# Attention over experts: output projection and value projection each go one head later, directly in front of a block of value products

## The chip, the cores and the metric

One core of one Trainium2 chip runs the whole program. The metric is the device time of one execution in microseconds (us), the median of three runs. The profile is one further execution with the hardware profiler on. In it PE is TensorE (PEld its weight loads), DVE is VectorE, ACT is ScalarE, POOL is GpSimd and SP is SyncE, which issues the DMAs.

## What is computed

A network of four layers on 16 sequences of 256 tokens with 128 features; each layer is an attention and a feed-forward part, each behind a layer normalisation and added to `x`. Three of these parts are attentions with 16 heads of 8 features: that of layer 1, the feed-forward part of layer 2 (four expert attentions on the same tokens, each with its own weights, a mask of the tokens that chose it, and a gate), and the attention of layer 3 (with rotary tables). Cut to that, for one sequence and one set of weights:

```python
q, k, v = (x @ wq + bq), (x @ wk + bk), (x @ wv + bv)      # per head of 8 features
att = softmax(mask(einsum('bqhd,bkhd->bhqk', q, k) * scale))
y = einsum('bhqk,bkhd->bqhd', att, v).reshape(b, s, d)
out = out.at[...].add(gate * (y @ wo + bo))                # four experts: one such term each
```

## The kernel before

`attention8` carries out these three attentions: once for layer 1 (16 jobs, one for each sequence), and once for layers 2 and 3 together (64 jobs, sequence times expert, then 16 late jobs of layer 3). A job is one sequence under one set of weights. The five engines each run a list of steps; in step `at` an engine works on several jobs at different depths, and `s.has(off)` asks whether job `at + off` exists. A step goes over 16 heads, `u` = 0 to 15.

On PE, each head of a step gives one pair of matmuls of scores for job `at + 1` (`scores_part`, L596, into `psS`) and, beside them, one pair of transposed, shifted scores (`shifted_part`, L603, into `psT`), all on 49 or 51 rows of the array. DVE takes the row maxima of each `psS` bank (`maxima`, L831), ACT the exponentials of each `psT` bank (`exponential`, L754). `psS` and `psT` have three banks each (`SCORE_BANKS, SHIFTED_BANKS, MISC_BANKS = 3, 3, 1`), used in turn, so before a head's pair PE waits until the maxima and the exponentials of the head three before it are done (`max_done`, `exp_done`, L616 and L622).

Between the heads stand larger blocks of PE, at places written out by hand in `step` (L692 on): the projections to q and k after head 0 (L582, L583), the turning of the output after head 3 (L664), four blocks of value products `prob_values(s, 0..3)` after heads 3, 6, 10 and 14 (L645, 16 matmuls each that write 32-column strips of the array), the turning of the maxima after head 4 (L671) and of y after head 6 (L679), the output projection `project_out` after head 9 (L686 for the bias, L689), and the value projection `project_v` after head 13 (L589). When late jobs are underway, a second projection follows head 3 and one more transpose ends the step.

All the blocks except the value products write one shared PSUM bank in a fixed order: q and k, o, m, y, out, v. Each of them waits until the previous one was taken out (`misc_taken`, in `fill`, L571). `add_output` on DVE (behind the maxima of head 10) takes the output projection: two instructions at L855 for the expert jobs, one at L859 for the others. `write_values` on ACT (behind the exponential of head 13) takes the value projection; a POOL copy of tokens (`tokens`, L953) waits for that, and the q projection of the next step waits for the copy. SP's queue and POOL's other steps wait for none of the two projections.

PE takes its matmuls in the order of its list, and so do DVE, ACT and POOL with theirs: an instruction that waits holds up all behind it.

Of the kernel before, what the change touches and what calls it, by code (L numbers as in the profile page):

```python
# [414 lines left out]
def attention8(nc, m, name, w, weights=1, masked=False, then=None):  # L415
# [12 lines left out]
    with ExitStack() as ctx:  # L428
# [45 lines left out]
        def of(s, off):  # L474

            return then if s.late(off) else w
# [89 lines left out]
        def _(pe):  # L566
# [7 lines left out]
            def project_qk(s, kind, wq, wk):  # L574
                if s.late(3) and then:
                    wait_taken(pe, s, "n", 3)
                    xc = m.xT16[:, s.batch(3), :]
                else:
                    pe.wait_ge(tokens_ready, s.n(3, 1, 1))
                    xc = xcur[:, s.quarter(3), :]  # L580
                ps, full = fill(s, kind, 3)
                pe.matmul(ps[:, 0:SEQ], wq[:, s.expert(3), :], xc, start=True, stop=True)  # L582
                pe.matmul(ps[:, SEQ:2 * SEQ], wk[:, s.expert(3), :], xc, start=True, stop=True).then_inc(full, 1)  # L583
# [22 lines left out]
            def score_pair(s, u):  # L606

                off, h = shifted_head(u)
                if s.has(1):
                    if u == 0:  # L610
                        if s.at == -1:
                            norm.wait(pe, GROUPS - 1)
                        pe.wait_ge(stack_ready, s.n(1, stack_inc, stack_inc))
                    back = score_bank(s, u)[1]
                    if s.known(1, 1) or u >= back:
                        pe.wait_ge(max_done, s.n(1, HEADS, u + 1 - back))  # L616
                if s.has(off):
                    if h == 0:
                        pe.wait_ge(maxrow_ready, s.n(0, 32, 32))
                    back = shifted_bank(s, u)[1]  # L620
                    if s.known(off, 1) or h >= back:
                        pe.wait_ge(exp_done, s.n(off, HEADS, h + 1 - back))  # L622
                for t in range(2):
                    if s.has(1):
                        a = scores_part(s, u, t)
                        if t == 1:
                            a.then_inc(scores_ready, 1)
                    if s.has(off):
                        b = shifted_part(s, u, t)
                        if t == 1:  # L630
                            b.then_inc(shifted_ready, 1)
# [26 lines left out]
            def turn_output(s):  # L658
                pe.wait_ge(oT_ready, s.n(-2, 2, 2))
                ps, full = fill(s, "o", -2)  # L660
                for t in range(2):
                    for half in range(2):
                        c = (2 * t + half) * P
                        mm = pe.transpose(ps[:, c:c + P], oT[:, half, t * P:(t + 1) * P], m.identity[:, :])  # L664
                mm.then_inc(full, 1)

            def turn_max(s):
                pe.wait_ge(negmax_ready, s.n(0, 1, 1))
                ps, full = fill(s, "m", 0)
                for t in range(2):  # L670
                    mm = pe.transpose(ps[0:2 * HEADS, 0:P].bitcast(BF16)[:, t * P:(t + 1) * P],  # L671
                                      negmax[:, t, :, :, :].rearrange("p g a h -> p (g a h)"), m.identity_bf[:, :])
                mm.then_inc(full, 1)

            def turn_y(s):
                wait_taken(pe, s, "o", -2)
                ps, full = fill(s, "y", -2)
                for t in range(2):
                    mm = pe.transpose(ps[:, t * P:(t + 1) * P], y[:, t, :], m.identity[:, :])  # L679
                mm.then_inc(full, 1)  # L680
# [11 lines left out]
            def step(s):  # L692
                for u in range(HEADS):
                    score_pair(s, u)
                    if u == 0 and s.has(3):
                        project_qk(s, "qk", of(s, 3).wq, of(s, 3).wk)
                    if u == 3 and s.has(3) and then and s.late(3):
                        project_qk(s, "qk2", then.wq2, then.wk2)
                    if u == 3 and s.has(-2):
                        turn_output(s)  # L700
                    if u == 3 and s.has(-1):
                        prob_values(s, 0)
                    if u == 4 and s.has(0):
                        turn_max(s)
                    if u == 6 and s.has(-1):
                        prob_values(s, 1)
                    if u == 6 and s.has(-2):
                        turn_y(s)
                    if u == 9 and s.has(-2):
                        project_out(s)  # L710
                    if u == 10 and s.has(-1):
                        prob_values(s, 2)
                    if u == 13 and s.has(0):
                        project_v(s)
                    if u == 14 and s.has(-1):
                        prob_values(s, 3)

                if then and s.has(5) and s.late(5):
                    turn_late(s)
                for g in groups_at.get(s.at, ()):  # L720
                    norm.turn(pe, g)
                if masked and s.at == -3:
                    route.project(pe)
                if masked and s.at == -2:
                    route.count(pe)
# [5 lines left out]
        def _(act):  # L731
# [48 lines left out]
            def copy_yT(s):  # L780
                ps, taken = wait_full(act, s, "y", -2)
                if s.known(-2, 1):
                    wait_taken(act, s, "out", -3)
                act.activation(yT[:, :], ps[:, 0:SEQ], ACT.Copy).then_inc(taken, 1)

            def step(s):
                for u in range(HEADS):
                    if u == 1 and s.has(-2):
                        copy_oT(s, -2, 1)
                    if u == 1 and s.has(3):  # L790
                        copy_qk(s, "qk", 0)
                    if u == 4 and s.has(3) and then and s.late(3):
                        copy_qk(s, "qk2", 1)
                    if u == 6 and s.has(0):
                        copy_max(s)
                    if u == 7 and s.has(-1):
                        copy_oT(s, -1, 0)
                    if u == 7 and s.has(-2):
                        copy_yT(s)
                    exponential(s, u)  # L800
                    if u == 7 and then and s.at in STATS_AT:
                        late_roots(STATS_AT.index(s.at))
                    if u == 13 and s.has(0):
                        write_values(s)

                if s.at == -4:
                    norm.root(act)
                if then and s.has(5) and s.late(5):
                    ps, taken = wait_full(act, s, "n", 5)
                    act.activation(m.xT16[:, s.batch(5), :], ps[:, 0:SEQ], ACT.Copy).then_inc(taken, 1)  # L810
                for g in groups_at.get(s.at, ()):
                    norm.keep(act, g)
                if masked and s.at == -3:
                    route.keep_logits(act)
                if masked and s.at == -2:
                    route.keep_mask(act)
# [5 lines left out]
        def _(dve):  # L822
# [95 lines left out]
            def step(s):  # L918
                for u in range(HEADS):
                    if s.has(1):  # L920
                        maxima(s, u)
                    if then and s.at in STATS_AT:
                        late_statistics(STATS_AT.index(s.at), u)
                    if u == 12 and then and s.has(5) and s.late(5):
                        late_normalise(s)
                    if u == 2 and s.has(-2):
                        normalise(s)
                    if u == 10 and s.has(-2):
                        add_output(s)
                    if u == 15 and s.has(-2) and (s.late(-2) or s.expert(-2) == weights - 1):  # L930
                        output_stats(s)

                if s.at == -4:
                    norm.statistics(dve)
                if masked and s.at == -4:
                    for g in range(GROUPS):
                        norm.normalise(dve, g)
                    route.choose(dve)
                elif not masked:
                    for g in groups_at.get(s.at, ()):  # L940
                        norm.normalise(dve, g)
# [1171 lines left out]
```

## Time and profile before

| | us |
|---|---|
| median of three runs | 2327.8 |
| the three runs | 2325.37 to 2330.94 |
| profiled execution, its own time | 2331.32 |
| its span, first to last instruction | 2329.6 |
| PE busy | 2085.3 (90%) |
| DVE busy | 1814.9 (78%) |
| ACT busy | 1460.6 (63%) |
| POOL busy | 695.9 (30%) |
| mean granted clock of TensorE | 0.954 |

The profiled execution took 3.5 us more than the median, and 1.7 us of it lie around the span. The layer-1 attention runs from about 590 to 812 us of the span, that of layers 2 and 3 from about 1079 to 2160 us. A busy PE in this profile is not PE at its peak, since the ends of matmuls are modelled; their starts are what to read.

### The profile page before, as it was taken

To read this page: it belongs to the slowest core of one execution; us is meant where nothing else is said; L and a number is where in the kernel's file an instruction comes from. 1 tells how busy PE (TensorE), PEld (TensorE's weight loads), DVE (VectorE), ACT (ScalarE), POOL (GpSimd) and SP (SyncE) were. 2 spreads that over 40 slices of the span, in tenths; PEclk is the share of its full clock that TensorE was granted. 3 is DMA by queue.
4 is the path that set the end of the run, shared out by engine and by line. 5 is a ranking of instruction groups with operands and counts; after the bars stand their busy time and mean duration, and the time that the engine had idled before them with its cause. 6 is when DMAs were issued, how large, how long until landed. Compare 5 with 4: busy or idle time off the path is not lost. (4 is left out here: it accounts for less than half of the span.)

```text
span 2329.6 us, 66565 instructions
## 1 busy us (share of the span) xinstructions
PE 2085.3 (90%) x21573; PEld 1237.6 (53%) x21573; DVE 1814.9 (78%) x4556; ACT 1460.6 (63%) x3730; POOL 695.9 (30%) x1221
## 2 busy tenths in 40 slices
PE   5999999987899887756999999999999888888798
PEld 4777777755355454542545555555555444444355
DVE  7878877755689647986889998899999877776564
ACT  3565555632488723322878888888888777777331
POOL 2111111100343101322434434434433355552110
PEclk9999999998799988776999999999999999999899
DMA  5000000000434100003343443444344333331000
GB/s 164 2 2 2 2 2 2 2 1 15 137 124 128 40 1 1 1 0 97 121 129 124 129 131 124 128 132 131 128 129 132 113 98 111 98 102 53 1 19 19
DMA packets 198398, 167.48 MB, mean 72 GB/s; under 512 B 15445, under 2 KB 178198, under 8 KB 198198
## 3 DMA queue, kind: packets, MB, share of 16 engines
q1 hardware_dynamic: 198198, 164.90, 22.4%
q8 instruction: 114, 1.87, 0.3%
q14 instruction: 86, 0.70, 0.1%
HBM read 85.42 MB, written 77.63 MB: 70 GB/s over the span
## 5 line engine op out<-in xcount | busy, mean ns | idle before, releaser
L831 DVE TENSOR_REDUCE a_rowmax<-a_psS 128x2 f32<-128x512 f32 x1536 | 964.1, 681 | 141.4 <-PE a_psS L596 137.0
L754 ACT ACTIVATE a_probs<-a_psT 128x512 f32<-128x512 f32 x1536 | 830.5, 601 | 228.9 <-PE a_psT L603 228.8
L596 PE MATMUL a_psS<-stackk,stackq 49*128 49x256 bf16 x3072 | 498.2, 278 | 46.6 <-DMA stackq<-a_negmaxT 14.2
L603 PE MATMUL a_psT<-stackq,stackk 51*128 51x256 bf16 x3072 | 481.9, 273 | 2.1 <-ACT a_probs L754 1.9
L645 PE MATMUL a_psO<-a_probs,values 128*32 128x256 f32 x6144 | 412.8, 386 | 1.4 <-ACT a_probs L754 1.4
L596 PEld LDWEIGHTS a_psS<-stackk,stackq 49*128 49x128 bf16 x3072 | 220.1, 95 | 296.8 <-DVE a_rowmax L831 116.5
L645 PEld LDWEIGHTS a_psO<-a_probs,values 128*32 128x32 f32 x6144 | 160.8, 109 | 144.8 <-issue 51.2
L1175 ACT ACTIVATE a_probs<-a_psS,a_negmax 128x256 f32<-128x256 f32 x256 | 121.1, 473 | 182.8 <-DVE a_negmax L1199 182.8
L603 PEld LDWEIGHTS a_psT<-stackq,stackk 51*128 51x128 bf16 x3072 | 216.9, 94 | 19.3 <-ACT a_probs L754 8.1
L1059 POOL TENSOR_TENSOR a_vr<-a_v,a_rsum 128x256 f32<-128x256 f32 x128 | 79.8, 623 | 392.3 <-DVE a_rsum L1260 371.9
L953 POOL COPY a_xcur<-xT 128x256 f32 (+1 forms) x80 | 31.7, 396 | 467.8 <-ACT values L778 371.7
L1197 DVE CUSTOM_DVE_ANT_0 a_psS<-a_psS,causal 128x256 f32<-128x256 f32 x256 | 114.4, 447 | 72.3 <-PE a_psS L1081 60.3
L982 POOL TENSOR_TENSOR a_parts<-a_rest,a_parts 128x512 bf16<-128x512 f32 x96 | 111.1, 1158 | 17.3 <-POOL a_parts L980 17.3
L992 POOL TENSOR_SCALAR a_negmax<-a_rowmax 128x16 bf16<-128x16 f32 x192 | 45.0, 252 | 232.2 <-DVE a_rowmax L831 180.4
L978 POOL TENSOR_TENSOR a_rest<-a_raw,a_parts 128x512 f32<-128x512 f32 x80 | 92.6, 1157 | 14.8 <-POOL a_parts L976 14.8
L1077 PE MATMUL a_psS<-a_qT,a_kT 64*128 64x256 f32 x512 | 90.5, 429 | 5.3 <-DVE a_qT L1208 2.9
L1177 ACT ACTIVATE a_probs<-a_psS,a_negmax 128x128 f32<-128x128 f32 x256 | 93.4, 365 | 0.0
L664 PE MATMUL a_shared<-identity,a_oT 128*128 128x128 f32 x384 | 62.2, 285 | 32.9 <-ACT a_raw L744 29.3
L1412 DVE TENSOR_TENSOR f_hidden<-f_silu,f_up 128x512 f32<-128x512 f32 x48 | 32.9, 685 | 73.5 <-ACT f_silu L1393 73.5
L1393 ACT ACTIVATE f_silu<-f_gate 128x512 f32<-128x512 f32 x48 | 28.7, 597 | 94.5 <-PE f_up L1365 94.5
L1091 PE MATMUL a_psQ<-xT,l_wq 128*64 128x256 f32 x512 | 84.0, 406 | 1.0 <-PEq L154 1.0
L1199 DVE CUSTOM_DVE_ANT_0 a_psS<-a_psS,causal 128x128 f32<-128x128 f32 x256 | 84.4, 330 | 0.0
(305 smaller groups left out, 3892.6 us busy)
## 6 DMA issues: line engine op xcount, KB each, us to landing
a_scratch<-a_parts SPq DMA_DIRECT2D x192, 192.0 KB, 2.4
stackq<-a_scratch SPq DMA_DIRECT2D x192, 192.0 KB
stackk<-a_scratch SPq DMA_DIRECT2D x192, 192.0 KB
a_scratch<-a_parts SPq DMA_DIRECT2D x192, 128.0 KB, 2.3
a_scratch<-a_parts SPq DMA_DIRECT2D x192, 64.0 KB, 1.9
stackq<-a_negmaxT SPq DMA_DIRECT2D x192, 8.0 KB
x<-in_x SPq DMA_DIRECT2D x4, 512.0 KB, 6.4
out<-x SPq DMA_DIRECT2D x8, 256.0 KB, 2.3
```

The lines of the kernel that those rows point to most:

```text
L596: return pe.matmul(psS[score_bank(s, u)[0]][:, t * SEQ:(t + 1) * SEQ], stackq[r:r + MAX_ROW, b, pr, t * P:(t + 1) * P], stackk[r:r + MAX_R ...
L603: return pe.matmul(psT[shifted_bank(s, u)[0]][:, t * SEQ:(t + 1) * SEQ], stackk[r:r + ZERO_ROW, b, pr, t * P:(t + 1) * P], stackq[r:r + ZE ...
L645: mm = pe.matmul(psO[SLOT * j:SLOT * (j + 1), half, :], values[:, s.parity(-1), t, VALUE_AT + SLOT * (8 * i + 4 * half + j) - 9 * i:VALUE_ ...
L754: act.activation(probs[:, h, :], psT[shifted_bank(s, u)[0]][:, :], ACT.Exp, scale=of(s, off).exp_scale).then_inc(exp_done, 1)
L831: dve.tensor_reduce(rowmax[:, s.parity(1), u, :], psS[score_bank(s, u)[0]][:, :].rearrange("p (t k) -> p t k", t=2), AX_X, ALU.max).then_i ...
L978: pool.tensor_tensor(rest[:, :, :], whole, parts[:, :, 0, :], ALU.subtract).then_inc(rest_ready, 1)
L982: pool.tensor_tensor(parts[:, :, 2, :], rest[:, :, :], parts[:, :, 1, :], ALU.subtract).then_inc(parts_ready, 1)
L1077: pe.matmul(psS[a][h][:, 0:SEQ], kT[r, a, 0:P], qT[r, a, :], start=True, stop=True, tile_position=(64 * h, 0), skip_group_check=True)
L1175: act.activation(probs[:, a, h, 0:SEQ], psS[a][h][:, 0:SEQ], ACT.Exp, scale=-1.0, bias=negmax[:, a, 2 * h:2 * h + 1], accum_out=sums[:, a, ...
L1177: act.activation(probs[:, a, h, SEQ:384], psS[a][h][:, SEQ:384], ACT.Exp, scale=-1.0, bias=negmax[:, a, 2 * h + 1:2 * h + 2], accum_out=su ...
L1197: dve.tensor_tensor_reduce(out=psS[a][h][:, 0:SEQ], in0=psS[a][h][:, 0:SEQ], in1=m.causal[:, :], scale=-1.0, scalar=-NEG, op0=ALU.add, op1 ...
L1199: dve.tensor_tensor_reduce(out=psS[a][h][:, SEQ:384], in0=psS[a][h][:, SEQ:384], in1=m.causal[:, 0:P], scale=-1.0, scalar=-NEG, op0=ALU.ad ...
```

## The change

Three calls on PE, ACT and DVE move one head later. `project_out` moves from behind head 9 to behind head 10, where `prob_values(s, 2)` follows it in the same turn of the loop. `project_v` moves from behind head 13 to behind head 14, where `prob_values(s, 3)` follows it. The two readers move with them: `write_values` behind the exponential of head 14, `add_output` behind the maxima of head 11. No instruction is added or removed, and the shared bank's order stays.

```diff
@@ -706,11 +706,11 @@
                         prob_values(s, 1)
                     if u == 6 and s.has(-2):
                         turn_y(s)
-                    if u == 9 and s.has(-2):
+                    if u == 10 and s.has(-2):
                         project_out(s)
                     if u == 10 and s.has(-1):
                         prob_values(s, 2)
-                    if u == 13 and s.has(0):
+                    if u == 14 and s.has(0):
                         project_v(s)
                     if u == 14 and s.has(-1):
                         prob_values(s, 3)
@@ -800,7 +800,7 @@
                     exponential(s, u)
                     if u == 7 and then and s.at in STATS_AT:
                         late_roots(STATS_AT.index(s.at))
-                    if u == 13 and s.has(0):
+                    if u == 14 and s.has(0):
                         write_values(s)
 
                 if s.at == -4:
@@ -925,7 +925,7 @@
                         late_normalise(s)
                     if u == 2 and s.has(-2):
                         normalise(s)
-                    if u == 10 and s.has(-2):
+                    if u == 11 and s.has(-2):
                         add_output(s)
                     if u == 15 and s.has(-2) and (s.late(-2) or s.expert(-2) == weights - 1):
                         output_stats(s)
```

## Rows read from the trace of the kernel before

**Rows 1.** Busy time by stretch (two answers): stretch, its length, each engine's busy us, PEclk, DMA.

```profile
core 0: us, PE busy (x) PEld busy (x) DVE busy (x) ACT busy (x) POOL busy (x), PEclk, DMA share, GB/s
1500.00:1512.20 12.20, 11.98 (x149) 6.40 (x149) 11.09 (x22) 10.38 (x24) 4.86 (x10) 1.00 0.42 130
...
1840.00:2090.00 250.00, 219.23 (x2510) 118.37 (x2506) 193.83 (x381) 188.32 (x421) 131.75 (x190) 1.00 0.33 104
```

**Rows 2.** Timeline of PE, heads 7 to 15: start, length, operation, count.

```profile
1504.03 0.28 PE L596 MATMUL a_psS<-stackk,stackq 49*128 49x256 bf16 x1
1504.14 0.27 PE L596 MATMUL a_psS<-stackk,stackq 49*128 49x256 bf16 x1
...
1504.59 0.27 PE L596 MATMUL a_psS<-stackk,stackq 49*128 49x256 bf16 x1
1504.79 0.28 PE L686 MATMUL a_shared<-l_bo_parts,ones_bf 128*128 128x256 bf16 x1
1504.91 0.61 PE L689 MATMUL a_shared<-l_wo,a_yT 128*128 128x128 f32 x4
1505.45 0.28 PE L596 MATMUL a_psS<-stackk,stackq 49*128 49x256 bf16 x1
...
1505.57 0.27 PE L596 MATMUL a_psS<-stackk,stackq 49*128 49x256 bf16 x1
...
1505.77 1.07 PE L645 MATMUL a_psO<-a_probs,values 128*32 128x256 f32 x16
1506.78 0.28 PE L596 MATMUL a_psS<-stackk,stackq 49*128 49x256 bf16 x1
...
1507.37 0.27 PE L596 MATMUL a_psS<-stackk,stackq 49*128 49x256 bf16 x1
...
1507.57 0.71 PE L589 MATMUL a_shared<-l_wv,a_xcur 128*128 128x128 f32 x4
1508.22 0.28 PE L596 MATMUL a_psS<-stackk,stackq 49*128 49x256 bf16 x1
...
1508.54 1.07 PE L645 MATMUL a_psO<-a_probs,values 128*32 128x256 f32 x16
1509.54 0.28 PE L596 MATMUL a_psS<-stackk,stackq 49*128 49x256 bf16 x1
```

**Rows 3.** Timeline of DVE in the same stretch.

```profile
1504.45 0.69 DVE L831 TENSOR_REDUCE a_rowmax<-a_psS 128x2 f32<-128x512 f32 x1 [0.48 <-PE a_psS L596]
...
1506.85 0.60 DVE L855 SCALAR_TENSOR_TENSOR x<-a_shared,gate,x 128x128 f32 x2
1507.37 0.68 DVE L831 TENSOR_REDUCE a_rowmax<-a_psS 128x2 f32<-128x512 f32 x1
```

**Rows 4.** Timeline of PE in narrow looks: last output matmul, last transpose, value products.

```profile
1505.24 0.28 PE L689 MATMUL a_shared<-l_wo,a_yT 128*128 128x128 f32 x1
...
1500.37 0.27 PE L664 MATMUL a_shared<-identity,a_oT 128*128 128x128 f32 x1
...
1500.57 0.42 PE L645 MATMUL a_psO<-a_probs,values 128*32 128x256 f32 x4
```

**Rows 5.** Timelines of PE and DVE, step 1 of layers 2 and 3 (no output yet).

```profile
1112.72 0.28 PE L596 MATMUL a_psS<-stackk,stackq 49*128 49x256 bf16 x1
...
1113.28 0.27 PE L596 MATMUL a_psS<-stackk,stackq 49*128 49x256 bf16 x1
1113.92 0.27 PE L596 MATMUL a_psS<-stackk,stackq 49*128 49x256 bf16 x1 [0.37 <-DVE a_rowmax L831]
...
1113.15 0.69 DVE L831 TENSOR_REDUCE a_rowmax<-a_psS 128x2 f32<-128x512 f32 x1 [0.17 <-PE a_psS L596]
```

**Rows 6.** One line's instructions, all 32 of them: min/median/max ns, first and last start.

```profile
L859 DVE TENSOR_TENSOR x<-a_shared,x x32: 384/412/425, 636.2 to 2162.3; 128x256 f32<-128x256 f32 x24, 128x256 f32 x8
```

**Rows 7.** Timelines of ACT, POOL and PE, same step: value projection's way on.

```profile
1504.49 2.06 ACT L754 ACTIVATE a_probs<-a_psT 128x512 f32<-128x512 f32 x4
...
1508.68 0.42 ACT L778 ACTIVATE values<-a_shared 128x256 f32<-128x256 f32 x1
...
1509.44 0.40 POOL L953 COPY a_xcur<-xT 128x256 f32 x1 [5.11 <-ACT values L778]
...
1510.09 0.70 PE L582 MATMUL a_shared<-a_xcur,l_wq 128*128 128x256 f32 x2
```

**Rows 8.** Who waited for whom, whole run: us in total, times, longest.

```profile
PE a_psS L596 <- DMA stackq<-a_negmaxT: 14.2, 12, 3.1
```

**Rows 9.** Timeline of PE: waits for the shared bank, in two late steps in sequence.

```profile
1929.97 0.63 PE L664 MATMUL a_shared<-identity,a_oT 128*128 128x128 f32 x4 [1.09 <-ACT a_raw L744]
...
1945.26 0.63 PE L664 MATMUL a_shared<-identity,a_oT 128*128 128x128 f32 x4 [1.09 <-ACT a_raw L744]
```

## The prediction

> **What bounds the kernel now.** I read the stretches first, then the timeline of PE in one step of the layer-2 loop, then DVE and ACT in the same 12 us, and last the waits of the whole run. The stretches show a step of 12.20 us in which PE is busy for 11.98 us, DVE for 11.09 and ACT for 10.38 [rows 1]. So PE sets the pace, but DVE is only 0.9 us behind it and any time in which DVE starves is near to being on the path. PE runs at the full 2.4 GHz (granted 1.00), and still does in the late steps, where it is busy for 219 of 250 us [rows 1] with waits as long as 1.09 us in them [rows 9]; so short waits of PE, such as I expect below, don't bring the clock down.
>
> The timeline of PE [rows 2] is to be read by starts. I count from the first score matmul of head 7 (1504.03) and call the heads H7, H8 and so on. Three heads (H7, H8, H9) stand together; the last matmul of H9 starts at 0.56. Then the bias of the output projection at 0.76, the projection itself at 0.88, H10 at 1.42, value products at 1.74, H11 at 2.75. Again three heads stand together (H11, H12, H13, the last at 3.34), then the value projection at 3.54, H14 at 4.19, value products at 4.51, and H15 at 5.51. Nothing in it is a wait for a bank. Note the group size: three heads, and there are three banks.
>
> DVE [rows 3] starts the maxima of H7 at 0.42, after 0.48 us of waiting for PE: it has nothing left to do when H7 arrives. That instruction ends at 1.11 (0.42 + 0.69). The maxima of H8, H9, H10 follow without a gap; then the two L855 instructions fill 2.82 to 3.42, and the maxima of H11 start at 3.34.
>
> **The change part by part.**
>
> *What it removes: one change of tile shape for each move.* Between two score matmuls of a group lie 0.11 us from start to start (1504.03 to 1504.14 [rows 2]). Where the kind of matmul changes, it is about 0.20: H9's last to the bias 0.20, H10's last to the value products 0.20 [rows 2], the last output matmul (1505.24) to H10 0.21 [rows 2, 4]. The order "projection, then value products" has a row too, in the block after head 3: the last transpose on the full array starts at 1500.37 and the value products at 1500.57, again 0.20 [rows 4]. So before: 0.20 (H9 to projection) + 0.21 (projection to H10) + 0.20 (H10 to products) = 0.61. After: 0.11 (H9 to H10) + 0.20 (H10 to projection) + 0.20 (projection to products) = 0.51. Each move gives back 0.10 us of PE, two of them 0.20 us in a step.
>
> The Trainium skill says the same of this place: TensorEngine Tiling (Array Packing), section Key Properties, has "Changing tiling mode (not just tile) drains the TensorE". The trace agrees with about 0.1 us for a change. By that rule alone the kernel would get faster; this is my first rival.
>
> *What it adds: a fourth head in a group of three banks.* After the change H10 comes directly behind H9. PE could issue it at 0.67 (0.56 + 0.11), but its bank is that of H7, and the maxima of H7 end only at 1.11. DVE can't have them earlier, since it starts them as soon as H7 is there. The trace before has this very order in step 1, where no output exists yet and heads 7 to 10 stand together [rows 5]: H7 starts at 1112.72, H9's last at 1113.28, DVE starts at 1113.15 and ends at 1113.84, and H10 starts at 1113.92, 1.20 after H7 and 0.08 after the end of its maxima, with the wait put down to DVE. I take 1.20. The exponentials free the other bank no later (ACT starts four of them at 0.46, about 0.6 each [rows 7], so the first ends near 1.06). What waits behind H10 on PE is everything: projection, products, H11.
>
> *The new timetable, first half.* H10 at 1.20, its second matmul at 1.31; bias at 1.51 (+0.20); projection at 1.63 (+0.12), its last matmul at 1.96 (+0.33, from 1504.91 to 1505.24); products at 2.16 (+0.20); H11 at 3.17 (+1.01, as 1505.77 to 1506.78). Before, H11 came at 2.75: **+0.42**. The 0.66 us of projection used to cover the wait for H7's maxima; now nothing does.
>
> *Second half.* DVE has finished H10's maxima by about 2.9 (0.42 + 4 x 0.6) and starves until H11 is there. The output's reader, which used to fill that hole, now stands behind H11's maxima. These start at 3.59 (3.17 + 0.42) and end at 4.28. H14 needs that bank: 4.36 (+0.08), while PE was ready for it near 3.87. Its second matmul is at 4.48 (+0.12), and the value projection could start at 4.68 (+0.20). But it writes the shared bank, which is free only when DVE's reader is through: L855 starts at 4.19 (3.59 + 0.60, the pace of the maxima), takes 0.60 for the two [rows 3], ends at 4.79, and lets the value projection go at 4.87 (+0.08). Value products 0.65 later (as v to H14 now, 1507.57 to 1508.22) at 5.52, H15 1.00 later at 6.52. Before it was 5.51: **+1.01 us a step**. Where the reader is the single L859, 0.41 us [rows 6], it ends at 4.60, the value projection goes at 4.68, just as PE is ready, and H15 comes at 6.33: **+0.82 us a step**.
>
> *From H15 on* the order is the old one, all of it shifted. Two things could be late next. The q projection waits for the token copy on POOL, which waits for ACT to take v. Now: v at 1507.57 (last matmul near 1508.0), ACT takes it at 1508.68, behind other exponentials, for 0.42; POOL copies at 1509.44 for 0.40; q starts at 1510.09, 0.25 after the copy's end [rows 2, 7]. After: v at 4.87 is complete about 0.7 later; ACT, whose exponential of H14 starts at about 5.1 and runs for 0.6, takes it at about 5.65, to 6.07; POOL (+0.34) copies from 6.41 to 6.81; PE is ready for q at 7.07 (6.52 + 0.55, as 1509.54 to 1510.09). So it is hidden with some 0.2 us to spare; uncovered it costs what it overruns, to be bounded by one more exponential ahead of it, 0.5 us minus those 0.2, in each step. On ACT only the exponential of H15 stands behind the moved reader, and it waits for H15 anyway. On DVE the maxima of H12 to H14 stand behind L855; H15 needs H12's maxima, which end near 5.5, in time. No DMA is issued by what moves; SP and the other steps of POOL only follow the shift.
>
> *What it gives back.* Head 12 now and then waits for the DMA that brings the maxima, 12 times in the run, 14.2 us together [rows 8]. Heads 12 come 0.42 later, so up to 12 x 0.42 = 5 us of these vanish (bounds 0 and 14.2; I take 5).
>
> *The sum.* Steps with both moves and scores: 13 for layer 1 (steps 2 to 14, L859), 64 with an expert's output (steps 2 to 65, L855), 13 late ones (66 to 78, L859). 64 x 1.01 + 26 x 0.82 = 86 us, less 5: **+81 us**. The profiled execution would go from 2331.3 to 2412; it was 3.5 us above the median, so the median goes from 2327.8 to **2409 us**.
>
> The Trainium skill points this way also: Perfetto Trace Analysis, section Optimization Strategy, reads the same gap repeating on the engine that should be saturated as a sign of too little PSUM for the next tile. The trace before shows that gap only in a step such as that of rows 5.
>
> **The rivals.**
>
> *Faster by the saved tile changes alone.* If H7's maxima were done when PE reaches H10, 90 steps x 0.20 = 18 us would be gained: 2310 us. For it: the 0.20 rows. Against it: DVE would have to end 0.5 us sooner than it does, and it starts when H7 arrives. It decides from the point where the wait for a bank is under 0.10 us at each place.
>
> *Only the first wait counts.* If the later start of H11 gives DVE time to be ahead at H14 and the output is read in time, a step loses 0.42 - 0.10 = 0.32: 29 us, less 5: 2352. Against it: DVE starves before H11, so H11's maxima can't be early.
>
> *No change.* The waits would have to go where PE waits anyhow. In the loop that is 0.22 us of 12.20 [rows 1]; the late steps have more, but in front of H4, ahead of the moves. Against it is all of the timetable.
>
> *More than forecast.* The way v, values, tokens, q overruns by 0.3 us a step: 90 x 0.3 = 27 more, 2436.
>
> **How the numbers follow.** Forecast (both waits, 2378 to 2430) 0.80; first wait alone 0.06; overrun 0.05; faster 0.05; no change 0.04. The range: without the wait for L855 all steps would cost 0.82, 90 x 0.82 - 5 = 69, 2397; with all 14.2 us of the DMA waits gone too, 60, 2388; I go 10 further down for waits that overlap in part. Upward, with no DMA wait saved 2414, and 0.18 us a step for half of the overrun, 16, gives 2430. So 2378 to 2430. Faster by over 0.2% (about what a measurement can tell, 4.7 us) 0.05, within it 0.04, slower 0.91.
>
> **What would show it.** Right: on PE a wait of about 0.5 us in front of H10's and H14's scores, put down to the maxima of H7 and H11; DVE idle for about 0.6 us in front of H11's maxima; projections that start 0.20 after a score and products 0.20 after a projection; the value projection waiting for L855; steps of about 13.2 us in the loop and about 16.1 in late steps (15.29 now, 1929.97 to 1945.26 [rows 9]). Wrong: H10 less than 1 us after H7, or H15 less than 6 us after H7. If the bank waits are there but the step isn't longer, the timetable missed a slack; if steps are above 13.4, look at the token copy.

## The result, and the profile after

The changed kernel takes 2397.67 us (median of 4 runs, 2395.80 to 2399.49), the kernel before 2328.23 us beside it (median of 4 runs, 2325.37 to 2330.94): 1.0306 times as long, 95% interval 1.0291 to 1.0320. That is 69.4 us slower; the forecast was 2409 us, 81 us slower, in a range of 2378 to 2430. The profiled execution took 2397.04 us with a span of 2395.3, so it went up by 65.7 us against the profiled execution of before. Its mean clock is the same (0.955 after, 0.954 before).

The first look is at one step of the layer-2 loop in the stretches view of the changed kernel (length, then busy us of PE, PE's weight load, DVE, ACT and POOL, then the granted clock, the DMA share and GB/s). It answers to [rows 1]:

```profile
core 0: us, PE busy (x) PEld busy (x) DVE busy (x) ACT busy (x) POOL busy (x), PEclk, DMA share, GB/s
1502.00:1515.25 13.25, 12.16 (x150) 6.67 (x150) 11.24 (x22) 10.46 (x24) 5.10 (x10) 1.00 0.38 121
```

The step has become 1.05 us longer, and PE, DVE and ACT are busy in it for nearly what they were. PE's idle time rose from 0.22 to 1.09 us. So nothing got dearer: PE waits, at full clock.

Where it waits stands in the timeline of PE in that step (start, length, operation, and in brackets the idle time before it and who ended it). It answers to [rows 2], from the first score matmul of H7 at 1506.04 on:

```profile
1506.04 0.28 PE L596 MATMUL a_psS<-stackk,stackq 49*128 49x256 bf16 x1
...
1506.60 0.27 PE L596 MATMUL a_psS<-stackk,stackq 49*128 49x256 bf16 x1
...
1507.24 0.27 PE L596 MATMUL a_psS<-stackk,stackq 49*128 49x256 bf16 x1 [0.37 <-DVE a_rowmax L831]
...
1507.35 0.27 PE L596 MATMUL a_psS<-stackk,stackq 49*128 49x256 bf16 x1
...
1507.57 0.28 PE L686 MATMUL a_shared<-l_bo_parts,ones_bf 128*128 128x256 bf16 x1
1507.69 0.61 PE L689 MATMUL a_shared<-l_wo,a_yT 128*128 128x128 f32 x4
1508.23 1.07 PE L645 MATMUL a_psO<-a_probs,values 128*32 128x256 f32 x16
1509.23 0.28 PE L596 MATMUL a_psS<-stackk,stackq 49*128 49x256 bf16 x1
...
1510.43 0.27 PE L596 MATMUL a_psS<-stackk,stackq 49*128 49x256 bf16 x1 [0.37 <-DVE a_rowmax L831]
...
1510.92 0.71 PE L589 MATMUL a_shared<-l_wv,a_xcur 128*128 128x128 f32 x4
1511.56 1.07 PE L645 MATMUL a_psO<-a_probs,values 128*32 128x256 f32 x16
1512.57 0.28 PE L596 MATMUL a_psS<-stackk,stackq 49*128 49x256 bf16 x1
...
1513.11 0.70 PE L582 MATMUL a_shared<-a_xcur,l_wq 128*128 128x256 f32 x2
```

Read it by starts. H9's last score matmul stands at 0.56 after H7's first, H10 at 1.20: a gap of 0.64 us where 0.11 would do, so 0.53 us lost (the bracket says 0.37, since it counts from the modelled end of the matmul before). H14 has the same gap (from 1509.80, left out above, to 1510.43). Both waits are put down to the maxima. The value projection begins 0.38 after H14's last matmul (1510.54, left out above) instead of 0.20: that is the wait for DVE's reader of the output.

The same step on DVE, as [rows 3]:

```profile
1506.47 2.48 DVE L831 TENSOR_REDUCE a_rowmax<-a_psS 128x2 f32<-128x512 f32 x4 [0.48 <-PE a_psS L596]
1509.66 0.69 DVE L831 TENSOR_REDUCE a_rowmax<-a_psS 128x2 f32<-128x512 f32 x1 [0.71 <-PE a_psS L596]
1510.27 0.60 DVE L855 SCALAR_TENSOR_TENSOR x<-a_shared,gate,x 128x128 f32 x2
1510.78 1.88 DVE L831 TENSOR_REDUCE a_rowmax<-a_psS 128x2 f32<-128x512 f32 x3
```

DVE does four maxima and then sits idle for 0.71 us before H11's, where the two L855 instructions used to stand; they now come behind H11's maxima, and the value projection waits for them.

Over the whole run the waits have changed so (engine and line that waited, who ended it: us in total, times, longest). First the kernel before, then the changed one:

```profile
PE a_psS L596 <- DVE a_rowmax L831: 11.4, 19, 1.3
PEld a_shared L589 <- DVE x L855: 9.9, 47, 0.2
PE a_psS L596 <- issue: 4.7, 6, 1.9
```

```profile
PE a_psS L596 <- DVE a_rowmax L831: 74.5, 190, 0.9
PEld a_shared L589 <- DVE x L855: 23.2, 64, 0.4
PE a_psS L596 <- DMA stackq<-a_negmaxT: 4.5, 2, 2.5
PE a_psS L596 <- issue: 0.5, 2, 0.4
```

Two waits a step in some 90 steps make most of the 190; 19 were there before. The third line after answers to [rows 8]: 14.2 us of waits for the DMA became 4.5.

### The profile page after: what moved, and what is told of

It is laid out like the page before. It is cut to its first block and busy times, and to the rows that moved or that the text cites. A ratio compares the mean times of both kernels' runs of the same rounds, so it can differ in the third digit from the quotient of the medians.

```text
span 2395.3 us, 66551 instructions
## 1 busy us (share of the span) xinstructions
PE 2096.1 (88%) x21559; PEld 1244.0 (52%) x21573; DVE 1822.0 (76%) x4556; ACT 1460.9 (61%) x3730; POOL 698.3 (29%) x1221
## 5 line engine op out<-in xcount | busy, mean ns | idle before, releaser
L754 ACT ACTIVATE a_probs<-a_psT 128x512 f32<-128x512 f32 x1536 | 815.4, 600 | 298.6 <-PE a_psT L603 298.6
L596 PE MATMUL a_psS<-stackk,stackq 49*128 49x256 bf16 x3072 | 491.8, 277 | 94.1 <-DVE a_rowmax L831 74.5
L603 PE MATMUL a_psT<-stackq,stackk 51*128 51x256 bf16 x3072 | 477.0, 273 | 4.9 <-ACT a_probs L754 4.7
L596 PEld LDWEIGHTS a_psS<-stackk,stackq 49*128 49x128 bf16 x3072 | 225.7, 95 | 359.6 <-DVE a_rowmax L831 172.2
L664 PE MATMUL a_shared<-identity,a_oT 128*128 128x128 f32 x384 | 62.2, 285 | 32.9 <-ACT a_raw L744 28.9
```

The source lines that it names most:

```text
L596: return pe.matmul(psS[score_bank(s, u)[0]][:, t * SEQ:(t + 1) * SEQ], stackq[r:r + MAX_ROW, b, pr, t * P:(t + 1) * P], stackk[r:r + MAX_R ...
L603: return pe.matmul(psT[shifted_bank(s, u)[0]][:, t * SEQ:(t + 1) * SEQ], stackk[r:r + ZERO_ROW, b, pr, t * P:(t + 1) * P], stackq[r:r + ZE ...
L754: act.activation(probs[:, h, :], psT[shifted_bank(s, u)[0]][:, :], ACT.Exp, scale=of(s, off).exp_scale).then_inc(exp_done, 1)
```

## The experiments

The theory: each move puts four heads in front of three banks, so PE waits for the maxima (twice a step), and the late reader of the output adds a third wait. Every kernel was timed together with the kernel before, which stood at 2328.1 to 2328.4 us.

**One part at a time.** The first takes the changed kernel and gives DVE's reader its old place:

```
-                    if u == 11 and s.has(-2):
+                    if u == 10 and s.has(-2):
                         add_output(s)
```

> The changed kernel with add_output put back behind the maxima of head 10, so that the output's reader on DVE runs in the hole in front of head 11's maxima. My theory (the value projection waits for L855 through the shared bank): its start comes 0.18 us earlier in each of 64 steps, 0.20 behind head 14's last score instead of 0.36; 64 x 0.18 = 12 us less than the changed kernel's 2397.7, so 2386. The two bank waits in front of heads 10 and 14 stay. Rival (the value projection is held by something else): no difference, 2398.

It took 2387.04 us (1.0251, 1.0224 to 1.0279), about 11 us less than the changed kernel. On DVE the L855 pair fills the hole again, in front of the maxima of H11 (timeline of DVE):

```profile
1506.39 0.60 DVE L855 SCALAR_TENSOR_TENSOR x<-a_shared,gate,x 128x128 f32 x2
1507.18 2.48 DVE L831 TENSOR_REDUCE a_rowmax<-a_psS 128x2 f32<-128x512 f32 x4 [0.19 <-PE a_psS L596]
```

No wait of the value projection for L855 is left, and the waits for the banks are untouched (74.7 us, 190 times). So the late reader costs about 11 us, and the rest is the banks.

The second moves only the output projection, from the kernel before:

```
-                    if u == 9 and s.has(-2):
+                    if u == 10 and s.has(-2):
                         project_out(s)
```

> The kernel before with the output projection alone moved behind head 10; add_output stays behind the maxima of head 10, the value projection stays behind head 13. My theory (head 10 waits for head 7's bank): head 11 comes 0.44 us later and nothing else waits, so H15 is 0.44 later than before in 90 steps, 40 us, less some 16 us of DMA waits in front of head 12 that vanish: 2352. Rival (the saved tile change decides, the bank wait is hidden): 90 x 0.10 less, 2319.

2350.72 us (1.0095, 1.0066 to 1.0124), so +22.6, as the theory has it. One wait a step appears, in front of H10 (timeline of PE, then the waits of the whole run):

```profile
1510.94 0.28 PE L596 MATMUL a_psS<-stackk,stackq 49*128 49x256 bf16 x1 [0.42 <-DVE a_rowmax L831]
```

```profile
PE a_psS L596 <- DVE a_rowmax L831: 43.0, 105, 1.3
```

The third moves only the value projection:

```
-                    if u == 13 and s.has(0):
+                    if u == 14 and s.has(0):
                         project_v(s)
...
-                    if u == 13 and s.has(0):
+                    if u == 14 and s.has(0):
                         write_values(s)
```

> The kernel before with the value projection and write_values alone moved behind head 14. My theory (head 14 waits for head 11's bank by itself): DVE has the maxima of head 11 done at 4.02 us after head 7, head 14 goes at 4.10 instead of 3.45, head 15 at 6.07 instead of 5.51: 0.56 us a step, 50 us in 90 steps, and head 12 comes no later within its step, so few DMA waits vanish: 2370 to 2378. Rival (head 14's wait arises only because head 11 is late in the changed kernel): 90 x 0.10 less, 2319.

2358.53 us (1.0132, 1.0106 to 1.0157), so +30.4: the mechanism was right, the size was not. The wait stands in front of H14 (again the timeline of PE and the waits of the whole run):

```profile
1508.18 0.28 PE L596 MATMUL a_psS<-stackk,stackq 49*128 49x256 bf16 x1 [0.50 <-DVE a_rowmax L831]
```

```profile
PE a_psS L596 <- DVE a_rowmax L831: 46.8, 97, 1.1
PE a_psS L596 <- DMA stackq<-a_negmaxT: 8.5, 6, 3.6
```

Most steps of the loop grew by 0.57 us, as the expectation worked out (0.56). But the 26 steps with L859 grew by 0.45 only. In every fourth step of the loop a wait of 0.28 us in front of H0 went away, which comes from the turn of the loop ("The steps", below). And H12 was held up by 9.8 us in all by starts, where before it was 24.7 ("The give-back", below). Adding up: 22.6 + 30.4 + the 11 of the reader = 64 of the 69.4 us.

**The readers' time.** If the wait is for the maxima, shorter maxima must make it shorter. Two kernels, one from each side, let DVE and ACT read half of each bank (the expectation says what is left out):

```
-   act.activation(probs[:, h, :], psT[...][:, :], ...)
+   act.activation(probs[:, h, 0:SEQ], psT[...][:, 0:SEQ], ...)
...
-   dve.tensor_reduce(rowmax[...], psS[...][:, :].rearrange("p (t k) -> p t k", t=2), ...)
+   dve.tensor_reduce(rowmax[...], psS[...][:, :].rearrange("p (t k) -> p t k", t=2)[:, :, 0:P], ...)
```

> The kernel before with half of the work per score bank on its two readers: the maxima are taken over half of the keys, and the exponential is taken for half of the columns (the value products read that half twice). PE's work and every wait stay. Every theory: the step is paced by PE, so 2315 to 2330.

> The changed kernel with the same halved maxima and exponentials. My theory (head 10 and head 14 wait until the readers have left the bank): the maxima take about 0.41 us, the exponential about 0.39; head 10 goes at about 0.97 after head 7 instead of 1.20, head 15 at about 6.02 instead of 6.53, so a step costs 0.51 more than before instead of 1.01 (0.38 instead of 0.82 where L859 reads): 64 x 0.51 + 26 x 0.38 = 42 us over half_before, less up to 10 us of DMA waits: 32 to 42 over it. Rival (the new neighbourhood on PE costs the time, not the readers): as between the whole kernels, 69 us over half_before.

They took 2307.23 us (0.9921, 0.9898 to 0.9944) and 2348.67 us (1.0094, 1.0073 to 1.0115). The first came out lower than the 2315 to 2330 expected: most steps of its loop take 12.21 us as before, but the wait in every fourth step is gone, late steps take 15.07 instead of 15.28, and H12 is late by 17 us in all instead of 24.7. The difference, 41.4 us, is in the range of the theory (32 to 42) and far from the 69 that the change would have cost if the readers' time didn't matter. The second of them in the timelines of PE and of DVE (H7 at 1502.26):

```profile
1503.25 0.27 PE L596 MATMUL a_psS<-stackk,stackq 49*128 49x256 bf16 x1 [0.16 <-DVE a_rowmax L831]
```

```profile
1502.69 1.42 DVE L831 TENSOR_REDUCE a_rowmax<-a_psS 128x2 f32<-128x256 f32 x4 [1.16 <-PE a_psS L596]
```

H10 comes 0.99 after H7 instead of 1.20, and the wait is 0.16 instead of 0.37. DVE waits for 1.16 us before these maxima, so it is far from busy, and PE waits for it all the same. What counts is the time from a head's scores to the end of its maxima, not DVE's load. In the changed kernel that is 0.43 us until the maxima start and 0.69 for them, and H10 follows 0.08 later. These two runs don't tell the two readers apart, since both were halved. The traces do in part: the exponential that frees the other bank ends 0.06 us before the maxima, so by these rows shorter maxima alone could gain no more than that at each wait, an estimate that no run tests.

**The DMA's share.** H12 needs the maxima that a DMA brings. ACT copies them out at head 6; at head 5 the DMA starts earlier. From the kernel before, and from the changed one:

```
-                    if u == 6 and s.has(0):
+                    if u == 5 and s.has(0):
                         copy_max(s)
```

> The kernel before with one change of another kind: ACT copies the maxima (copy_max) in front of the exponential of head 5 instead of head 6, so that SP sends them some 0.45 us earlier. My theory (in the kernel before, head 12 often waits for that DMA, and the changed kernel lost less than I had summed because its head 12 comes later): these waits vanish here too, 14 to 18 us less than before, 2312. Rival (the waits are of the DMA's load and not of its start, or other steps take them over): 2328.

> The changed kernel with copy_max in front of the exponential of head 5, as in max_copy_early. My theory (the changed kernel has almost no waits left for the DMA in front of head 12, which is why it lost 69 us and not 81): nothing to gain, 2397, and it stands 79 us over max_copy_early, which is the price of the bank waits without that give-back. Rival (the copy helps wherever it is): 10 us less than the changed kernel, 2388.

From the kernel before it gives 2318.09 us (0.9958, 0.9943 to 0.9973): about 10 us faster than before, and the fastest kernel of this study that does all the work. The waits of this kernel:

```profile
PE a_psS L596 <- DVE a_rowmax L831: 9.3, 18, 1.0
PE a_psS L596 <- DMA stackq<-a_negmaxT: 8.8, 7, 2.8
PE a_psS L596 <- issue: 1.8, 4, 0.8
```

These three lines fell by 2.1, 5.4 and 2.9 us, 10.4 together. The direction was right, the size (2312 expected) too large, since 7 of the 12 DMA waits stayed. From the changed kernel the same edit gives 2395.58 us (1.0301, 1.0278 to 1.0324), nothing beyond the measurement: there the later H12 has already taken the gain. Against the better kernel the change therefore costs 77.5 us.

**Is the saved change of tile shape to be had at all?** The same neighbourhood (projection directly in front of products) can be made the other way, by taking the products one head earlier, so that the groups stay at three heads:

```
-                    if u == 10 and s.has(-1):
+                    if u == 9 and s.has(-1):
                         prob_values(s, -1, 2)
-                    if u == 13 and s.has(0):
+                    if u == 12 and s.has(0):
                         project_v(s)
-                    if u == 14 and s.has(-1):
+                    if u == 13 and s.has(-1):
                         prob_values(s, -1, 3)
...
-                    if u == 13 and s.has(0):
+                    if u == 12 and s.has(0):
                         write_values(s)
...
-                    if u == 10 and s.has(-2):
+                    if u == 9 and s.has(-2):
                         add_output(s)
```

> The kernel before with the value products moved to the output projection instead of the other way round: prob_values(2) directly behind project_out after head 9, project_v after head 12, prob_values(3) after head 13, add_output and write_values behind the maxima of head 9 and the exponential of head 12. The same change of tile is saved (one in a step: score, projection, products, score), but the groups of scores stay 3, 3, 1, 3 and no head waits for a bank. My theory (the bank, not the neighbourhood, costs the time): 90 x 0.10 = 9 us less than before, 2319, if the DMA of the maxima is in time; but head 12 comes about 0.15 us earlier in its step, so more waits for that DMA eat some of it: 2319 to 2330, with no step above 12.5 but for those waits. Rival (projections next to value products cost time in themselves, or the four turns about them disturb DVE): slower than before by half of the change, 2360.

> The same move of the value products, together with copy_max in front of head 5's exponential, so that the DMA in front of head 12 starts 0.45 us earlier. My theory: the saved tile change shows in full, 90 x 0.10 = 9 us less than copy_max alone (2318), so 2309, and faster than the kernel before by 0.8%. Rival (the step is bound by DVE or by the exchange through the shared bank as soon as PE gets shorter): no less than copy_max alone, 2318.

Alone it took 2338.69 us (1.0042, 1.0023 to 1.0061), with the earlier copy of the maxima 2328.70 us (1.0008, 0.9993 to 1.0022). Both miss: 10 us slower than without the move, where a gain was expected. The timeline of PE in the second says where the gain goes (its last line is of the kernel before, for the same place):

```profile
1502.70 0.28 PE L596 MATMUL a_psS<-stackk,stackq 49*128 49x256 bf16 x1
...
1508.62 0.70 PE L582 MATMUL a_shared<-a_xcur,l_wq 128*128 128x256 f32 x2
...
1510.94 0.66 PE L664 MATMUL a_shared<-identity,a_oT 128*128 128x128 f32 x4 [0.25 <-ACT a_raw L744]
...
1512.22 0.66 PE L664 MATMUL a_shared<-identity,a_oT 128*128 128x128 f32 x4 [0.25 <-ACT a_raw L744]
```

From H7 to the q projection it is 5.92 us, where before it was 6.06 [rows 2, 7]: 0.14 is saved. From q to the transpose at L664 it is 2.32, where before it was 2.13 (1510.09 to 1512.22). PE waits there for ACT's copies of q and k, and ACT is behind (timeline of ACT, same step):

```profile
1508.32 1.57 ACT L754 ACTIVATE a_probs<-a_psT 128x512 f32<-128x512 f32 x3 [0.38 <-PE a_psT L603]
1509.76 0.40 ACT L760 ACTIVATE a_oT<-a_psO 128x256 f32<-128x256 f32 x1
1510.03 0.50 ACT L744 ACTIVATE a_raw<-a_shared,l_bq 128x256 f32<-128x256 f32 x1
```

Three exponentials in a row, then a copy of the attention output, then q's copy. If that copy (L760) is in the way, it can be done at head 14 of the step before, ahead of its exponential:

```
-                    if u == 1 and s.has(-2):
-                        copy_oT(s, -2, 1)
...
+                    if u == 14 and s.has(-1):
+                        copy_oT(s, -1, 1)
```

> both_early with one more move: ACT copies the second half of the output (copy_oT) in front of the exponential of head 14 of the step before, where it waited 0.38 us for PE, and no longer behind the exponential of head 0, in front of the copies of q and k. My theory (both_early saves 0.14 us of PE from head 7 to the q projection, and gives 0.19 back where the turning of the output waits for ACT's copies): that wait shrinks by 0.17 or more, the step goes from 12.29 to about 12.12, 90 x 0.17 = 15 us less than both_early: 2313, 5 less than max_copy_early. Rival (the step then waits for DVE, which has 11.1 us of work in it): 2318 to 2328.

2326.25 us (0.9997, 0.9983 to 1.0010): as its rival says, no gain to speak of. The wait for ACT at L664 shrinks, from 31.0 us to 21.3, while the waits for the maxima stay about what they were, 18.4 and 20.2 (waits of the whole run of this kernel):

```profile
PE a_psS L596 <- DVE a_rowmax L831: 20.2, 45, 2.1
PE a_shared L664 <- ACT a_raw L744: 21.3, 32, 1.1
```

By starts, where no DMA wait disturbs them, two of four steps of the loop now take 12.10 us, 0.11 less than the 12.21 of the kernel with only the earlier copy of the maxima: there the saved change of tile shape does reach the step. The other two give it back. One takes 12.28, with H3 0.70 behind H2 instead of 0.32, put down to the maxima; the one in which the loop turns over ("The steps", below) takes 12.62 instead of 12.49, with H0 0.72 behind H15 instead of 0.51. So the mean is 12.28 in both kernels, and the saving that the expectation put in every step comes in two of four. The run is some 8 us longer all the same. Between the two profiled executions, which lie 13.0 us apart, 5.5 of it lie in layer 1 and 3.3 in the first steps of layers 2 and 3; what makes these longer was not settled. What the misses do show is that 0.1 us saved on PE at one place of this step can turn up as a wait for DVE or ACT, or at the turn of the loop. DVE and ACT have 11.1 and 10.4 us of work in a step of 12.2 [rows 1].

## Why the prediction was right, step by step

**The timetable.** It was worked out from starts, and held to 0.03 us. Forecast and measured, in us after H7: H10 1.20 and 1.20, H11 3.17 and 3.19, H14 4.36 and 4.39, the value projection 4.87 and 4.88, H15 6.52 and 6.53. The source of the first number was the one step of the kernel before in which four heads stood together [rows 5]; everything else follows from durations in [rows 2 and 3]. The prediction's other marks are there too: the hole in DVE, 0.71 us instead of 0.6; products 0.66 after the bias and 0.20 after the last matmul of the projection; no wait of q for the tokens. ACT took v at 5.63 (forecast 5.65), POOL copied at 6.20 (6.41) and q came at 7.07 (7.07), so the token copy stayed hidden.

**The steps.** Three of four loop steps grew by 1.05 to 1.09 (forecast 1.01). The 0.04 to 0.08 above are in part a wait that ended 0.13 us after the maxima instead of 0.08 in some steps; why was not settled. Every fourth step grew by 0.80 only. The program's loop on PE holds four steps, and where it turns over, 12 times in layers 2 and 3, H0 of the next step used to come late: 0.51 us behind H15, where other steps have 0.23. After the change it is 0.27 (first matmuls of H15 and of H0, step 43 of layers 2 and 3, before and then after):

```profile
1644.74 0.28 PE L596 MATMUL a_psS<-stackk,stackq 49*128 49x256 bf16 x1
...
1645.25 0.28 PE L596 MATMUL a_psS<-stackk,stackq 49*128 49x256 bf16 x1
```

```profile
1685.22 0.28 PE L596 MATMUL a_psS<-stackk,stackq 49*128 49x256 bf16 x1
...
1685.49 0.28 PE L596 MATMUL a_psS<-stackk,stackq 49*128 49x256 bf16 x1
```

In the trace the branch that turns PE's loop begins 0.15 us after the end of H13's maxima, before and after, and H0 starts 0.62 after the branch. H13 comes in because four steps have 64 heads, which three banks don't divide: in the last of them H15 takes the bank of H13, two heads back and not three, and so waits for its maxima. These end 0.26 us ahead of H15's start in the kernel before and 0.50 us ahead of it in the changed one, where most of the turn is hidden. The prediction had read one step and taken it for all 64. Steps with L859 grew by 0.88 (forecast 0.82). Together 52 x 1.07 + 12 x 0.80 + 26 x 0.88 = 88 us, against a forecast of 86: the errors cancel.

**The give-back.** This is the term that was mis-sized. It was put at 5 us with bounds of 0 and 14.2; measured it is 88 - 65.7 = 22, outside its own bounds. In the rows of waits those for the DMA fell by 9.7 us and those put down to issue by 4.2, which is 14. The rest lies in what these rows leave out, since a bracket counts from the modelled end of the matmul before. By starts, H12 stands 0.23 us behind H11 in an undisturbed step. In the 90 steps of the sum it stood later than that (by over 0.05) in 34 before, 24.7 us together, and in 8 after, 3.1 us together. That is 21.6 us less, the whole term within 1 us. Of H12's three conditions in the program, the maxima of H9 and an exponential end 0.6 us or more before H12 is due in 32 of the 34 steps, which leaves the DMA. The prediction took the 14.2 us of one row for all there was, and let each wait shrink by the 0.42 by which H12 is later, but waits of 1 to 2 us vanished whole.

One difference that the trace shows: from the end of ACT's copy of the maxima to H12 it was 3.57 us at the least before, and 4.00 after. That alone doesn't explain it. With the copy one head earlier, in the kernel before, it is 4.04 at the least, and H12 is still late in 21 steps, by 11.7 us. Why a wait of 2 us goes with a delay of 0.4 isn't shown. The total stayed in the range because the range was wide enough for this error, and that it lies on 2397, the prediction's figure without the wait for L855, is luck: that wait is there and costs about 11 us.

**The late steps.** Forecast 16.1 us, with L859 as the reader (15.29 + 0.82). The transposes at L664 in the changed kernel, in sequence, as [rows 9]:

```profile
1937.02 0.63 PE L664 MATMUL a_shared<-identity,a_oT 128*128 128x128 f32 x4 [1.09 <-ACT a_raw L744]
...
1953.34 0.63 PE L664 MATMUL a_shared<-identity,a_oT 128*128 128x128 f32 x4 [1.09 <-ACT a_raw L744]
```

It is 16.32 from one to the next, and the wait of 1.09 in front of them is as it was. These two steps still have an expert's output, so by the prediction's own terms they should take 15.29 + 1.01 = 16.30; later ones, with L859, take 16.17. The old wait couldn't take in the new waits, as the prediction said against the rival of no change.

**The rivals.** "Faster by the saved tile changes" decided from bank waits under 0.10 us; they are 0.53. The saved change itself is in the trace: the products start 0.20 behind the last projection matmul, and each move has one change of about 0.1 us less. The sentence of the Trainium skill (TensorEngine Tiling (Array Packing), Key Properties) that a change of tiling mode drains TensorE thus agrees with the rows, and the kernel gets slower all the same, since a wait of five times that price comes with it. "Only the first wait counts" fell at H14, where the second wait is as long as the first; the run with the value projection alone shows it by itself. "More than forecast" asked for a token copy that overruns; it doesn't. The Trainium skill (Perfetto Trace Analysis, Optimization Strategy) says that the same gap repeating can mean too little PSUM for the next tile, and the 190 waits agree in that each is for a bank of PSUM. But here the order of issue brought the gap, with the same number of banks, and the old order covers it.

## What to carry to other kernels

Count the banks against the tiles that are issued between two larger blocks of work. A block that looks as if it stood in the way may be what covers the wait for a bank, and with one tile more than there are banks in a group, the whole time from the matmul to the end of its reader comes to light, however idle the reader is. Read a whole turn of the program's loop, since one step may not stand for all. Look as well at where the reader of a moved product then stands in its own engine's queue. And a cheap look at the longest few waits, here those for one DMA, may bring more than the move itself: starting the copy ahead of it one head earlier gave 10 us of 2328.

## What the runs showed of the hardware

A matmul that waits for a bank started 0.05 to 0.14 us after the end of the instruction that freed it: H14 0.08 after the end of H11's maxima (1509.66 + 0.69 to 1510.43), the value projection 0.05 after L855 (1510.27 + 0.60 to 1510.92), H10 or H14 in other steps 0.13, and 0.14 with the halved readers. The spread was not expected and costs 0.05 us a step where the wait ends 0.13 after and not 0.08. A change of the tile shape costs some 0.1 us by starts (0.20 against 0.11), and leaves no idle row.

The transfer that brings the maxima is the least steady part of a step. In the kernel before, H12 came late in 22 of the 64 steps with an expert's output (by over 0.05 us by starts, 15.4 us together, at most 2.8), though the brackets that name the DMA show only 8 waits of 0.2 us or more in them (7.6 us). With H12 about 0.4 us later it was late in 3 (1.1 us), and with the transfer started about 0.5 us earlier in 12 (6.0 us).

The turn of a program's loop can stand on TensorE's path. H0 came 0.62 us after the branch in the kernel before, in the changed kernel and in the one with products and copy both early. Whether that is hidden depends on how long before H15 the wait in front of the branch ends: 0.26 us before leaves H0 0.28 late, 0.50 leaves 0.04, and 0.06, in the kernel with products and copy both early, leaves 0.50. No run takes the loop away.
